# Score banks, halves of the value product and router logits at the end of an attention kernel

## The reference

```python
h = _layernorm(x, axis=-1) * (1 + ca) + sa
scores = einsum('bnhd,bmhd->bnmh', q, k) / sqrt(d)
att = softmax(scores, axis=2)
x = x + ga * (einsum('bnmh,bmhd->bnhd', att, v).reshape(Bn, Nn, Dn) + h)
h = _layernorm(x, axis=-1) * (1 + cb) + sb
probs = softmax(h @ router_w.T, axis=-1)
topk_w, topk_idx = top_k(probs, 2)                  # weights sum to one
x = x + gb * (experts weighted by topk_w + shared)(h)
... (layer 1: the same frame around its own attention and feed-forward)
```

## Time and profile before

| What | us |
|---|---|
| Median of 3 runs (1047.33 to 1050.42) | 1047.78 |
| The profiled execution, as timed | 1047.59 |
| Its span in the profile | 1045.8 |
| TensorE busy, share of the span | 988.8, 95% |
| VectorE busy, share of the span | 857.4, 82% |
| ScalarE busy, share of the span | 675.3, 65% |
| GpSimd busy, share of the span | 307.4, 29% |
| Granted TensorE clock, mean over the span | 0.944 of full |
| All 1024 exponentials (line 1197) | 544.6 |
| All 480 reduces of maxima behind the first unit's (line 1419) | 576.9 |

### The profile page before, as it was taken

How to read it: one execution, slowest core, us unless ns; L and a number is a source line. 1 busy time by engine, 2 the same in 40 slices (tenths; PEclk the granted TensorE clock), 3 DMA queues, 4 the chain that set the end, 5 groups by cost and what they waited for, 6 DMA issues and landing times. The chain is left out here.

```text
span 1045.8 us, 19112 instructions
## 1 busy us (share of the span) xinstructions
PE 988.8 (95%) x6968; PEld 499.5 (48%) x6968; DVE 857.4 (82%) x1162; ACT 675.3 (65%) x1316; POOL 307.4 (29%) x347
## 2 busy tenths in 40 slices
PE   6998999999999999999999999999997889997867
PEld 5453433333333333333333333333456768996656
DVE  5488799999999999999999999987456464655786
ACT  2423777888888888888888888774753224553312
POOL 3285864000000221000000000047437620045553
PEclk8999899999999999999999999996898879997888
DMA  6799200033110110110111101300002224444211
GB/s 197 216 152 134 99 16 6 20 92 106 39 40 6 40 40 7 38 32 16 37 27 21 37 9 39 67 6 1 6 5 70 74 84 144 128 123 135 88 49 60
DMA packets 90129, 65.54 MB, mean 63 GB/s; under 512 B 48406, under 2 KB 77942, under 8 KB 89462
## 3 DMA queue, kind: packets, MB, share of 16 engines
q1 hardware_dynamic: 85334, 54.36, 21.8%
q0 software_dynamic: 3072, 8.39, 2.6%
q10 hardware_dynamic: 1632, 1.58, 0.5%
HBM read 34.93 MB, written 26.74 MB: 59 GB/s over the span
## 5 line engine op out<-in xcount | busy, mean ns | idle before, releaser
L1197 ACT ACTIVATE prob<-ps 128x512 f32<-128x512 f32 x1024 | 544.6, 599 | 127.7 <-PE ps L683 114.8
L1419 DVE TENSOR_REDUCE mxp<-ps 128x2 f32<-128x1024 f32 x480 | 576.9, 1220 | 22.2 <-PE ps L653 17.4
L683 PE MATMUL ps<-qst,kst 50*128 50x512 f32 x1024 | 374.6, 458 | 5.2 <-DMA qst<-nmT 3.5
L653 PE MATMUL ps<-kst,qst 48*128 48x512 f32 x960 | 328.3, 452 | 0.0
L683 PEld LDWEIGHTS ps<-qst,kst 50*128 50x128 f32 x1024 | 159.7, 190 | 255.2 <-ACT prob L1197 224.6
L724 PE MATMUL ps<-prob,vp 128*32 128x256 f32 x2464 | 196.8, 391 | 0.0
L653 PEld LDWEIGHTS ps<-kst,qst 48*128 48x128 f32 x960 | 130.6, 186 | 14.6 <-issue 6.5
L717 PE MATMUL ps<-prob,vp 128*32 128x512 f32 x816 | 115.6, 640 | 0.0
L724 PEld LDWEIGHTS ps<-prob,vp 128*32 128x32 f32 x2464 | 48.5, 108 | 113.6 <-issue 60.9
L2049 POOL TENSOR_TENSOR att_u<-o_x,rec 128x256 f32<-128x256 f32 x16 | 9.9, 620 | 224.4 <-DVE rec L1444 224.2
L1992 POOL CAST nmp<-nmx 128x16 fp32r<-128x16 f32 x16 | 3.1, 196 | 243.9 <-DVE nmx L1423 218.2
(11 more groups left out here) (262 smaller groups left out, 1250.9 us busy)
## 6 DMA issues: line engine op xcount, KB each, us to landing
qst<-q_parts SPq DMA_DIRECT2D x96, 64.0 KB, 2.6
xg<-x_slots SPq DMA_DIRECT2D x46, 128.0 KB
y_slots<-ysb SPq DMA_DIRECT2D x46, 128.0 KB
x_slots<-zero SPq DMA_DIRECT2D x10, 512.0 KB, 3.2
kst<-k_parts SPq DMA_DIRECT2D x18, 256.0 KB, 11.5
k_parts<-parts SPq DMA_DIRECT2D x8, 512.0 KB, 4.2
q_parts<-parts SPq DMA_DIRECT2D x8, 512.0 KB, 10.7
att_t<-att_u SPq DMA_DIRECT2D x256, 8.0 KB, 1.8
```

The lines of the kernel that those rows point to most:

```text
L653: last = nc.tensor.matmul(ps[:, 2 * p + b, :], qst[rows, g, a, P * j:P * (j + 1)], kst[rows, GP * g + a, CH * m:CH * (m + 1)], start=True, ...
L683: nc.tensor.matmul(ps[:, bank, :], kst[rows, GP * g + k // 2, P * t:P * (t + 1)], qst[rows, g, k // 2, :], start=True, stop=True).then_inc ...
L1197: nc.scalar.activation(prob[:, t % 2, k, :], ps[:, banks[((u * MT if len(banks) == 3 else 0) * G + G * t + k) % len(banks)], :], ACT.Exp, ...
L1419: nc.vector.tensor_reduce(own, ps[:, 2 * p:2 * p + 2, :], AX.X, ALU.max).then_inc(mx_read, 1)
```

## The change

- A constant RING4 is the count of score tiles from which four banks are used: that of step 11 of unit 14. From there on the order of the banks is 5, 6, 4, 3, on through unit 15, with no new start at that unit. The fourth score of the new order (count RING4 + 3, the first one in bank 3) waits until VectorE has read all maxima; later ones wait for the exponential four counts back. ScalarE's list follows the same banks.
- Unit 13 takes the value product in halves in steps 2 to 15, unit 14 in steps 2 to 10.
- logits(0) is issued token tile by token tile, six matmuls behind each of the steps 2 to 5 of unit 15, logits(1) behind each of the steps 10 to 13. turn1(1, 0) and (1, 1) stand one step earlier, behind steps 6 and 7.
- ScalarE's two router exponentials move from ahead of steps 4 and 12 to ahead of steps 7 and 15.
- VectorE normalises chunks 1 and 2 before it takes the logits of the chunk before, and makes their halves before the ranks.

```diff
--- before.py
+++ after.py
@@ -67,6 +67,7 @@
 QD = 32
 NQ = P // QD
 MAX_LOADS = 2 * NQ
+RING4 = (NU - 2) * G * MT + G * (MI - LEAD)
 
 
 def build(nc, x_in, wq, bq, wk, bk, wv, bv, routerT, gate_w, up_w, down_w, sg_w, sg_b, su_w, su_b,
@@ -325,6 +326,9 @@
         def x_cols(t, n=1):
 
             return x[:].rearrange("p t d -> p (t d)")[:, bass.ds(t * D, n * D)]
+
+        def score_bank(n):
+            return (4, 5, 6)[n % 3] if n < RING4 else (5, 6, 4, 3)[(n - RING4) % 4]
 
         END = TPC * (NC - 1)
 
@@ -654,7 +658,7 @@
                                             kst[rows, GP * g + a, CH * m:CH * (m + 1)], start=True, stop=True)
                 last.then_inc(mx_ps, 1)
 
-            def unit(u, g, ahead, first=False, beside=None, banks=(4, 5, 6), halved=()):
+            def unit(u, g, ahead, first=False, beside=None, halved=()):
 
                 pe.wait_ge(nm_in, (u + 1) * (16 * MAX_LOADS))
                 for t in range(MT):
@@ -670,17 +674,15 @@
                     pairs = v * (2 * MI) + 2 * i
 
                     def score(k):
-                        n = G * t + k
-                        done = u * (G * MT) + n
-                        bank = banks[(done if len(banks) == 3 else n) % len(banks)]
-                        if len(banks) == 3 and done >= 3:
+                        done = u * (G * MT) + G * t + k
+                        if done == RING4 + 3:
+                            pe.wait_ge(mx_read, NU * (2 * MI))
+                        elif done > RING4 + 3:
+                            pe.wait_ge(p_s, done - 3)
+                        elif done >= 3:
                             pe.wait_ge(p_s, done - 2)
-                        elif n >= len(banks):
-                            pe.wait_ge(p_s, done - len(banks) + 1)
-                        elif n == 0 and not first:
-                            pe.wait_ge(p_s, done)
                         rows = slice(HALF * (k % 2), HALF * (k % 2) + KR + NM)
-                        nc.tensor.matmul(ps[:, bank, :], kst[rows, GP * g + k // 2, P * t:P * (t + 1)],
+                        nc.tensor.matmul(ps[:, score_bank(done), :], kst[rows, GP * g + k // 2, P * t:P * (t + 1)],
                                          qst[rows, g, k // 2, :], start=True, stop=True).then_inc(sc_ps, 1)
 
                     def next_maxima(p):
@@ -769,7 +771,7 @@
             pe.wait_ge(q32_s, len(ITEMS) - EASY)
             unit(0, 0, 2, first=True)
 
-            for u in range(1, NU - 3):
+            for u in range(1, NU - 2):
                 unit(u, u % NG, 2, halved=range(2, MT) if u >= 2 else ())
 
             def turn(q, ft, bank, src):
@@ -786,13 +788,14 @@
             def hT_pair(part, k, c):
                 return (hT_hi[:, c, k, :], hT_lo[:, (c * KT + k) * CH:(c * KT + k + 1) * CH])[part]
 
-            def logits(c, bank, col):
-
-                pe.wait_ge(h_lo_s, KT * (c + 1))
-                pe.wait_ge(tables_s, 2)
-                if c:
-                    pe.wait_ge(lg_s, c)
-                for j in range(TPC):
+            def logits(c, bank, col, tiles=range(TPC)):
+
+                if 0 in tiles:
+                    pe.wait_ge(h_lo_s, KT * (c + 1))
+                    pe.wait_ge(tables_s, 2)
+                    if c:
+                        pe.wait_ge(lg_s, c)
+                for j in tiles:
                     n = 0
                     for k in range(KT):
                         tokens = slice(P * j, P * (j + 1))
@@ -800,9 +803,8 @@
                             last = nc.tensor.matmul(ps[:, bank, col + E * j:col + E * (j + 1)], a[:, tokens], b[:, k, :],
                                                     start=n == 0, stop=n == 3 * KT - 1)
                             n += 1
-                last.then_inc(lg_ps, 1)
-
-            unit(NU - 3, 1, 2)
+                if TPC - 1 in tiles:
+                    last.then_inc(lg_ps, 1)
 
             def beside_last_but_one(t):
                 if t == 15:
@@ -811,18 +813,18 @@
             def beside_last(t):
                 if t == 0:
                     turn1(0, 1)
-                if t == 2:
-                    logits(0, 2, 0)
-                if t in (7, 8):
-                    turn1(1, t - 7)
-                if t == 10:
-                    logits(1, 2, 32)
+                if 2 <= t < 6:
+                    logits(0, 2, 0, (t - 2,))
+                if t in (6, 7):
+                    turn1(1, t - 6)
+                if 10 <= t < 14:
+                    logits(1, 2, 32, (t - 10,))
                 if t in (13, 14):
                     turn1(2, t - 13)
 
-            unit(NU - 2, 2, 1, beside=beside_last_but_one)
-
-            unit(NU - 1, 3, 0, beside=beside_last, banks=(4, 5, 6, 3))
+            unit(NU - 2, 2, 1, beside=beside_last_but_one, halved=range(2, MI - LEAD))
+
+            unit(NU - 1, 3, 0, beside=beside_last)
 
 
             PASSES = ((0, 0), (0, 1), (1, 0))
@@ -1186,7 +1188,7 @@
                 act.wait_ge(lg_s, c + 1)
                 nc.scalar.activation(pr[:], lg[:], ACT.Exp).then_inc(exp_s, 1)
 
-            def unit(u, first, ahead, exps={}, banks=(4, 5, 6)):
+            def unit(u, first, exps={}):
                 for t in range(MT):
                     if t in exps:
                         router_exp(exps[t])
@@ -1194,14 +1196,12 @@
                         act.wait_ge(sc_ps, u * (G * MT) + G * t + k + 1)
                         if k == 0 and not (first and t < 2):
                             act.wait_ge(pv_s, u * MT + t - 1)
-                        nc.scalar.activation(prob[:, t % 2, k, :], ps[:, banks[((u * MT if len(banks) == 3 else 0) * G + G * t + k) % len(banks)], :], ACT.Exp,
+                        nc.scalar.activation(prob[:, t % 2, k, :], ps[:, score_bank(u * (G * MT) + G * t + k), :], ACT.Exp,
                                              scale=DH ** -0.5).then_inc(p_s, 1)
 
-            unit(0, True, 2)
-            for u in range(1, NU - 2):
-                unit(u, False, 2)
-            unit(NU - 2, False, 1)
-            unit(NU - 1, False, 0, exps={4: 0, 12: 1}, banks=(4, 5, 6, 3))
+            for u in range(NU - 1):
+                unit(u, u == 0)
+            unit(NU - 1, False, exps={7: 0, 15: 1})
 
             def gate_up_rounded(i):
 
@@ -1600,15 +1600,17 @@
             statistics(1, 1)
             dve.wait_ge(zero_in, 16 * ZERO_DMAS)
             dve.wait_ge(tables_s, 3)
-            router(0, 2, 0)
+            normalise(1, 1)
+            router_logits(0, 2, 0)
+            both_halves(1)
+            router_ranks(0)
             shares(0)
-            normalise(1, 1)
-            both_halves(1)
             statistics(1, 2)
-            router(1, 2, 32)
+            normalise(1, 2)
+            router_logits(1, 2, 32)
+            both_halves(2)
+            router_ranks(1)
             shares(1)
-            normalise(1, 2)
-            both_halves(2)
             leave_output(NU - 1)
             invert_sums(NU - 1)
             router(2, 2, 64)
```

## The result

| | before | after |
|---|---|---|
| Median, us (range, runs) | 1047.99 (1046.79 to 1050.42, 6) | 1055.58 (1046.34 to 1058.04, 6) |
| Ratio, with its 95% interval | | 1.0069 (1.0042 to 1.0095) |
| Span of the profiled execution | 1045.8 | 1056.2 |

The change makes the kernel slower, by 7.6 us. I had forecast 1041.3.

What follows compares the result with a forecast made beforehand. Attention was taken to run dense on TensorE until about 700 us, then to lose time to waits for VectorE and GpSimd, router logits and low clock. Gains 2.9 + 0 + 0 + 3.6 = 6.5 took 1047.8 to 1041.3 us; range 1037.0 to 1046.0.

Steps and rivals of the forecast that it cites:

- part 3: First logits in quarters, transposes at steps 6 and 7 of unit 15: nothing beyond the 2.9 us, covered by a 3.4 us wait.
- Part 4, the term of the clock: Second logits in quarters, steps 10 to 13 of unit 15: gain 5.3 us at high clock, less 1.7 for low clock, 3.6.
- rival B: Second quartet wholly at 1.2 GHz, 17.9 us against 15.4: 1047.4 us; or quarters worth nothing, 1044.9; chance 0.22.
- Behind attention: From turn1(2, 1) on, the shift passes on whole; VectorE's moved ranks and shares of chunk 1 cost 0, at most 1 us.
- The shift: Halves in units 13 and 14 complete the last unit's maxima 2.9 us sooner, and the chain behind moves by that.
- Rival A: No wait at turn1(0, 0), as all four normalisations finish before GpSimd's cast: 12.5 us gained, 1035.3 us; chance 0.07.
- Rival C: Quarters keep the clock at 1.2 GHz from step 2 to step 7 of unit 15 as well: 1054.8 us; chance 0.07.

Runs made afterwards that it cites:

- halves_banks: The kernel before with the halves and the four banks only: 1044.31 us, ratio 0.9964; repeated, 1046.26 us, 0.9993.
- halves_only: The kernel before with unit 13 and steps 2 to 10 of unit 14 in halves, nothing else: 1045.76 us, ratio 0.9985.
- filler: The change with sixteen unread matmuls in TensorE's wait ahead of the second logits' quarters: 1046.01 us, ratio 0.9981.
- leave_fill: filler with unit 15's output transpose and reciprocal ahead of chunk 1's ranks and shares on VectorE: 1041.96 us, ratio 0.9956.
- second_undone: The change with second logits in one lump, chunk 1's VectorE order and the second router exponential as in the kernel before: 1048.81 us, ratio 1.0003.
- changed_down: The whole change with GpSimd's `down_rounded` moved as in down_later: 1039.82 us, ratio 0.9925; repeated, 1043.90 us, 0.9958.
- down_later: second_undone with `down_rounded` behind gate_attention(14) and a wait for normalise(1, 1): 1038.54 us, ratio 0.9908; repeated, 1038.79 us, 0.9911.
- down_fill: down_later with sixteen unread matmuls ahead of its second logits, which stay in one lump: 1038.56 us, ratio 0.9931.

## Why the prediction was wrong

**Right.** Unit 13 at 39.93 us (forecast 39.95). turn1(0, 0) 2.8 us sooner (2.9), with a wait of 8.90 (8). Four banks worth nothing that shows (halves_banks against halves_only: 0.9964 and then 0.9993 against 0.9985, the same positions within 0.5 us in the first profile). A quarter step at full clock 2.42 us (2.38). TensorE's wait for hT_lo ahead of the second logits 3.92 us (3.4). It was named as the cover of part 3, and it is what starts the loss.

**Part 4, the term of the clock, is the first step that failed.** I took 1.7 us for it, from the spells of the earlier trace rows, with 3.7 as its end. The spell lasted 17.1 us, the whole second quartet. A slow quarter step measured 4.39 (forecast 4.2), and the quartet 17.9 us, which is rival B's number to the tenth; in filler and leave_fill, at full clock, it took 10.3 and 10.2, near the 10.1 that I had worked out for the high clock. Both ends were priced right and the choice between them was wrong. My argument against B was that "full slow steps leave TensorE without a hole, and the clock rose after each such stretch". The window shows TensorE busy for all of its 17.10 us and the clock at 0.50 to the end. How long a spell lasted before was no measure for other work in it. The Trainium skill, "TensorE: Matmul & The Clock Gate", section "HAM oscillation — how this bites in real kernels", says that matmuls behind a long wait start cold. The trace agrees at the first wait (low from 714.9, inside it) and nearly so at the second: there the first quarter, from 751.85, still ran at full clock, and the clock fell at 752.5, behind it. The price lay in how long it then stayed low.

**Behind attention, "0, with 1 us as the bound", is the second.** From turn1(2, 1) to gate_attention(15) it took 13.0 us where before had 8.3, 4.7 more. I had counted chunk 1's 4.6 us of ranks against 6 us of GpSimd's work and called them hidden. Beside that work they took 9.8 us: rows of 0.42 became 2.53 and 2.58, one of 0.19 became 1.08. The Trainium skill, "SBUF — State Buffer", section "Who interferes with whom", has the rule: a VectorE instruction with two inputs in SBUF contends with a GpSimd instruction that reads SBUF, and the contention is an exclusive lock. The trace agrees: the two slow operations start 0.13 us behind GpSimd's (773.42 and 773.29, 775.87 and 775.74) and end 0.3 us behind them. I had the like before me in the earlier trace rows, the normalisations of 3.74 and 9.03 us, without applying it to the rows that I moved.

**The shift** reached the second logits as 1.8 us and not as 2.9: add_attention(14) waited 13.00 us for its DMAs where the earlier trace rows have 12.06. That is one profile; in the change's repeat the wait was 12.55 and the second logits came 2.5 us sooner.

**In sum**, at turn1(2, 1) the forecast was 6.5 us sooner and it came 0.7 later, 7.2 us off: 6.1 from the clock (17.9 where the forecast had 11.8) and 1.1 from the short shift. Behind it came 5.8 more to the scatter, 4.7 of them from VectorE's order, and 1.0 more to the end. Forecast and result lie 14.3 us apart by the medians, and 14.0 by the profiles' positions. Rival A did not occur. Rival C had the size (1054.8) and the wrong place: the first quarters ran at full clock.

**Not settled**: what the first quarters and chunk 0's order are worth alone, why the clock fell over the first quarters in second_undone and not in the change, and why changed_down and its repeat (0.9925, 0.9958) differ by more than either's half interval.

## What to carry to other kernels

When an edit shortens a path, look at the wait that it leaves on TensorE: price all of the work behind it at the lower clock until a stretch of that very work is seen to bring the clock back: here quarters stayed slow for 17.1 us and more, a lump for 10.2. When VectorE's work is moved, price it by what GpSimd does in its new place, not by its old rows. And look first for a long GpSimd instruction that stands ahead of what everyone waits for: moving `down_rounded` into a wait for DMAs was worth 10 us in this kernel (second_undone to down_later), more than any part of the change.

## What the runs showed of the hardware

- Sixteen matmuls whose result nobody reads, put into a wait of TensorE, made the kernel about 9 us faster (1.0071 to 0.9981), with no other work moved. In down_fill, where VectorE set the pace behind it, the same filler gained nothing (0.9908 and 0.9931).
- Thin work (scores, value product, six matmuls of 8 columns) kept the clock at 1.2 GHz for 17.1 to 23.9 us at a stretch, in the change with TensorE busy for all 17.10; one lump of logits behind a like wait had 10.2 us.
- The clock fell without any wait too: in second_undone at 729.9, for 10.2 us, with TensorE busy ahead of it and through it.
- Six runs of the change spread over 11.7 us, and the fastest had a higher mean clock than the slowest (1046.34 us at 0.954, 1058.04 at 0.945). Its repeat shows no such order (1052.46 us at 0.948, 1057.15 at 0.950).
